# Softmax denominators in a fused attention and feed-forward kernel: one-hot matmuls replaced by row sums of exponentials taken on ScalarE

## What is computed

```python
def _L0_xattn_ref(q, k, v, wq, wk, wv, wo_w, wo_b):     # 16 heads of 32, window 128
    ...
    scores = jnp.einsum('bhnqd,bhnkd->bhnqk', qb, kband) * math.sqrt(dk)
    ...
    scores = jnp.where(valid[None, None], scores, neg)
    attn = jax.nn.softmax(scores, axis=-1)
    out = jnp.einsum('bhnqk,bhnkd->bhnqd', attn, vband)
    out = out.reshape(b, h, s, dk).transpose(0, 2, 1, 3).reshape(b, s, d)
    return jnp.einsum('bsd,ed->bse', out, wo_w) + wo_b
...
x = x + _L0_xattn_ref(_layernorm(x, axis=-1), ctx_1024, ctx_1024, ...)
x = x + _L0_ffn_ref(_layernorm(x, axis=-1), ...)         # 512 -> 2048 -> 512, quantised operands
```

## Time and profile before

| | |
|---|---|
| median of 3 runs | 1255.44 us (1254.12 to 1260.5) |
| the profiled execution | 1255.64 us |
| its span, first to last instruction | 1253.9 us |
| busy: PE, DVE, ACT, POOL | 1158.9, 985.8, 639.6, 367.9 us |
| granted TensorE clock, mean | 0.979 of full speed |

### The profile page before, as it was taken

How to read it: one execution, slowest core, us unless ns; L and a number is a source line. 1 busy time by engine, 2 the same in 40 slices (tenths; PEclk the granted TensorE clock), 3 DMA queues, 4 the chain that set the end, 5 groups by cost and what they waited for, 6 DMA issues and landing times.

```text
span 1253.9 us, 23541 instructions
## 1 busy us (share of the span) xinstructions
PE 1158.9 (92%) x7904; PEld 785.0 (63%) x7904; DVE 985.8 (79%) x2527; ACT 639.6 (51%) x1000; POOL 367.9 (29%) x540
## 2 busy tenths in 40 slices
PE   5789999999999999999999875999999979999997
PEld 5667877877887787787787653444444434444443
DVE  6779888889888888888988665666666678888885
ACT  5254355345335434533533443555556457777774
POOL 1136346345444624534554330000000030112320
PEclk9899999999999999999999887999999989999999
DMA  8463473465356347445534631455554400567662
GB/s 275 112 153 76 135 185 95 117 173 126 103 152 157 97 127 190 106 110 165 132 97 118 166 103 43 157 199 205 211 193 143 150 1 31 188 222 246 221 208 92
DMA packets 91592, 181.23 MB, mean 145 GB/s; under 512 B 12896, under 2 KB 22368, under 8 KB 91488
## 3 DMA queue, kind: packets, MB, share of 16 engines
q1 hardware_dynamic: 91488, 179.92, 48.1%
HBM read 81.30 MB, written 41.94 MB: 98 GB/s over the span
## 4 chain that ended last, share of the span: by engine, by line
DVE 36%; PE 35%; issue 25%; ACT 2%; DMA 1%; SPq 1%; POOL 0%; DVEq 0%; ACTq 0%; POOLq 0%
PE bank L787 17%; DVE bank L1059 7%; DVE roped L1085 3%; PE bank L505 3%; PE bank L506 3%; PE bank L507 3%; DVE bn L1020 3%; DVE rt L1082 3%; DVE rt L1083 3%; PE bank L594 2%; DVE row_max L1059 2%; DVE neg_max L1101 2%; PE bank L578 2%; DVE x_res L1052 1%; PE bank L517 1%
## 5 line engine op out<-in xcount | busy, mean ns | idle before, releaser
L1059 DVE CUSTOM_DVE_ANT_0 bank<-bank,mask 128x256 f32<-128x256 f32 x512 | 201.5, 454 | 63.7 <-PE bank L594 56.2
L787 PE MATMUL bank<-wout_int,g_hi 128*128 128x512 bf16 x512 | 195.7, 382 | 9.2 <-DVE g_lo L1332 9.2
L756 PE MATMUL bank<-qT_hi,win_int 128*128 128x512 bf16 x512 | 194.1, 379 | 1.6 <-DVE qT_lo L1250 1.4
L787 PE MATMUL bank<-wout_int,g_lo 128*128 128x512 bf16 x512 | 195.6, 382 | 0.0
L756 PE MATMUL bank<-qT_lo,win_int 128*128 128x512 bf16 x512 | 194.0, 379 | 0.0
L859 ACT ACTIVATE probs<-bank 128x512 f32<-128x512 f32 x256 | 142.5, 603 | 48.6 <-PE bank L621 44.2
L1377 POOL TENSOR_SCALAR_AFFINE_SELECT probs<-probs 128x256 f32<-128x256 f32 x256 | 109.6, 432 | 101.9 <-ACT probs L859 98.9
L1332 DVE TENSOR_TENSOR g_lo<-h_int,g_hi 128x512 f16<-128x512 f32 x128 | 103.7, 810 | 36.3 <-ACT g_hi L987 35.1
L594 PE MATMUL bank<-k_st,q_st 96*128 96x256 f32 x512 | 103.7, 309 | 19.7 <-DVE row_max L1059 11.6
L960 ACT ACTIVATE h_ring<-bank,b_in,g_scale 128x512 f32<-128x512 f32 x96 | 73.4, 779 | 75.7 <-PE bank L756 57.0
L1274 DVE TENSOR_REDUCE hmax<-h_ring 128x512 f32 (+1 forms) x96 | 63.2, 681 | 61.2 <-ACT h_ring L960 59.2
(11 more groups left out here) (148 smaller groups left out, 2783.3 us busy)
## 6 DMA issues: line engine op xcount, KB each, us to landing
hidden_scratch<-h_ring SPq DMA_DIRECT2D x96, 256.0 KB, 2.0
h_ring<-hidden_scratch SPq DMA_DIRECT2D x96, 256.0 KB, 2.9
k_st<-k_hi SPq DMA_DIRECT2D x128, 128.0 KB, 2.4
q_st<-q_hi SPq DMA_DIRECT2D x128, 128.0 KB, 2.4
xq<-x_scratch SPq DMA_DIRECT2D x16, 1024.0 KB, 6.0
x_ln<-in_x SPq DMA_DIRECT2D x16, 512.0 KB, 4.6
ctx_raw<-in_ctxT SPq DMA_DIRECT2D x16, 512.0 KB, 5.4
k_st<-k_lo SPq DMA_DIRECT2D x64, 128.0 KB, 2.5
```

Source lines behind the costliest of these rows:

```text
L756: mm = pe.matmul(bank[f % 4][:], win_int[:, c, f * P:(f + 1) * P], part[:, par, c], start=c == 0 and part is qT_hi, stop=c == KC - 1 and p ...
L787: mm = pe.matmul(bank[4 * par + u][:], part[:, f % 4, u * P:(u + 1) * P], wout_int[:, f], start=f == 0 and part is g_hi, stop=f == FC - 1 ...
L1059: dve.tensor_tensor_reduce(sc, sc, mask[:, (1 - qb) * P:(1 - qb) * P + S], 1.0, NEG, ALU.add, ALU.max, row_max[:, qb, n:n + 1]).then_inc(m ...
```

## The change

Three things are done. **The sums:** after the row maximum ACT takes the exponential of the first scores in place, one call for each half of the queries, with a running sum over the row into `den` (`sum_exp`, 32 calls a step); the first scores use four banks in place of two, and `denominators` and `hot` go. **The shares:** the 32 sums per row are inverted at once, `widen` copies each inverse 32 times (128x1024, into `roped`), and eight matmuls with the identity turn them (`shares`), now in the same step between `clump(1)` and the last four heads; ACT copies the shares instead of the output, and DVE multiplies straight from the output's bank at the end of the step. **The norm of x:** its chain (12 operations instead of 10, with the last one dropped into the norm) and the norm itself move to POOL, its moments to DVE's first part, after pair 4. The mask's constant, the sign of the maxima and the tables loaded follow.

```diff
+        first = [bank[i] for i in (0, 1, 6, 7)]
+        den_wide = roped[:].rearrange("p c s -> p (c s)").rearrange("p (q h r) -> p q h r", q=2, h=H)
# PE
             def x_transposes(j, s):
...
-                    wait(pe, den_done, j - 1)
+                    wait(pe, share_out, 2 * (j - 1))
...
-            def shares(j):
+            def shares(j, has_proj):
+                pe.wait_ge(den_done, j + 1)
+                if not has_proj:
+                    pe.wait_ge(wt_done, j)
                 for half in range(2):
-                    if half == 0:
-                        pe.wait_ge(den_done, j + 1)
-                    pe.wait_ge(oT_out, 2 * j + half + 1)
                     for a in range(2):
-                        mm = pe.matmul(pv_bank[half][:, a * S:(a + 1) * S], pick[:, 2 * half + a], den_r, start=True, stop=True)
+                        i = 2 * half + a
+                        for qb in range(2):
+                            mm = pe.matmul(q_bank[half][:, a * S + qb * P:a * S + (qb + 1) * P],
+                                           den_wide[:, qb, KC * i:KC * (i + 1)].rearrange("p h r -> p (h r)"), ident[:],
+                                           start=True, stop=True)
                     mm.then_inc(share_mm, 1)
...
             def scores(b, n):
...
+                elif n < 4:
+                    wait(pe, onorm, 2 * b)
                 else:
-                    pe.wait_ge(max_done, 2 * (H * b + n - 1))
+                    pe.wait_ge(sum_done, H * b + n - 3)
...
-            def denominators(b, i, kb, has_proj):
...
-                if has_o:
-                    tiles[2] += [lambda: shares(b - 1)]
-                    tiles[3] += [lambda: qk_tile(b + 1, "q", 0)]
...
+                    tiles[2] += [lambda: qk_tile(b + 1, "q", 0)]
+                    tiles[3] += [lambda: qk_tile(b + 1, "q", 1)]
+                    tiles[4] += [lambda: v_tile(b + 1, 0)]
+                    tiles[5] += [lambda: v_tile(b + 1, 1, range(2))]
+                    tiles[6] += [lambda: v_tile(b + 1, 1, range(2, KC))]
...
-                some(4)
-                max_transposes(b)
-                some(4)
-                for n, count in enumerate((1, 2, 2, 3, 1, 1, 1, 0, 1, 1, 1, 0, 1, 1, 0, 0)):
+                some(6)
+                max_transposes(b, has_proj)
+                some(6)
+                for n, count in enumerate((2, 2, 2, 2, 1, 1, 1, 1, 0, 0, 0, 0, 0, 0, 0, 0)):
                     scores_t(b, n, has_o)
                     some(count)
                     if n in (7, 11, 15):
-                        clump(b, par, n // KC - 1, has_proj)
+                        clump(b, par, n // KC - 1)
+                    if n == 11:
+                        shares(b, has_proj)
# ACT
+            def sum_exp(b, n):
+                act.wait_ge(max_done, 2 * (H * b + n + 1))
+                if n == 0:
+                    wait(act, den_chain, b)
+                for qb in range(2):
+                    sc = first[n % 4][:, qb * S:(qb + 1) * S]
+                    ins = act.activation(sc, sc, ACT.Exp, bias=row_low[:, qb, n:n + 1], scale=-1.0,
+                                         accum_out=den[:, qb, n:n + 1])
+                ins.then_inc(sum_done, 1)
...
             def step(b, par, has_c, has_o, has_proj, has_xt):
-                if has_proj:
-                    norm1(b + 1)
+                sums(0)
                 if has_proj:
                     xt_lead(b + 1, 0)
                     xt_lead(b + 1, 1)
+                sums(1)
+                sums(2)
+                sums(3)
                 if has_proj:
                     split_hi("k", b + 1)
+                sums(4)
                 if has_o:
                     ot_lead(b - 1, 0, has_proj)
                     ot_lead(b - 1, 1, has_proj)
+                sums(5)
                 if has_proj:
                     v_copy(b + 1, 1 - par, 0)
+                sums(6)
+                if has_proj:
                     v_copy(b + 1, 1 - par, 1)
+                sum_exp(b, 14)
                 max_copy(b, 0, slice(0, 2))
                 max_copy(b, 0, slice(2, KC))
+                sum_exp(b, 15)
                 for n in range(H):
                     softmax_exp(b, n)
...
-                    if n == 12:
-                        oT_copy(b, 0)
+                    if n == 13:
+                        share_copy(b, 0)
+                    if n == 14:
+                        share_copy(b, 1)
# DVE
             def invert(b):
-                dve.wait_ge(den_mm, NC4 * (b + 1))
+                dve.wait_ge(sum_done, H * (b + 1))
                 wait(dve, share_mm, 2 * b)
-                dve.reciprocal(den_r, den_bank[:, 0:S]).then_inc(den_done, 1)
+                dve.reciprocal(den_r[:], den[:]).then_inc(den_chain, 1)
+
+            def widen(b, has_proj):
+                dve.wait_ge(den_chain, b + 1)
+                if has_proj:
+                    dve.wait_ge(lo_done["q"], KC * (b + 2))
+                dve.tensor_copy(den_wide, den_r[:].rearrange("p q (h o) -> p q h o", o=1).to_broadcast([P, 2, H, DK])).then_inc(den_done, 1)
...
             def step(b, par, has_c, has_o, has_proj, has_xt):
...
-                if has_o:
-                    between[0] += [lambda: invert(b - 1)]
-                    between[5] += [lambda: normalise(b - 1, 0), lambda: normalise(b - 1, 1)]
...
+                if has_xt:
+                    between[4] += [lambda: ln1_moments(b + 2)]
...
+                invert(b)
...
                 quantise_win(b)
-                if has_xt:
-                    ln1(b + 2)
+                widen(b, has_proj)
                 if has_o:
                     residual(b - 1, 1)
                     ln2_moments(b - 1, 1)
+                normalise(b, 0)
+                if has_o:
                     largest(b - 1, 0)
                     largest(b - 1, 1)
+                normalise(b, 1)
# POOL
+            def norm1(j):
+                pool.wait_ge(ln1_chain, LN_SC * (j + 1))
+                for s in range(2):
+                    pool.tensor_scalar(x_ln[:, s], x_ln[:, s], mv[:, 0, s, 0:1], rstd[:, s:s + 1], ALU.subtract, ALU.mult).then_inc(ln1_norm, 1)
...
             def step(b, par, has_c, has_o, has_proj, has_xt):
+                if has_proj:
+                    norm1(b + 1)
                 if has_o:
                     bias_x(b - 1)
...
                     ot_rest(b - 1, 0)
                     ot_rest(b - 1, 1)
+                if has_xt:
+                    for _ in ln1_scale(b + 2):
+                        pass
                 for n in range(H):
                     band(b, n)
```

More of the change, by code:

```diff
@@ L73, in constants @@
     q, k = np.arange(S)[:, None], np.arange(S)[None, :]
-    mask = folded(folded(np.where(np.abs(q - k) <= WINDOW, 0.0, NEG).astype(np.float32), 0), 1)
+    mask = folded(folded(np.where(np.abs(q - k) <= WINDOW, 0.0, FAR).astype(np.float32), 0), 1)
     assert not mask[:P, :P].any() and not mask[P:, P:].any()
     mask = np.concatenate([mask[P:], mask[:P, P:]], 1)
-    hot = np.tile((np.arange(HOT) % NC4 == NC4 - 1).astype(np.float32), (P, 1))
-    row, col = np.arange(P)[:, None], np.arange(P)[None, :]
-    pick = np.stack([row == DK * (col // DK) + i for i in range(NC4)], 1).astype(np.float32)
     sel = np.zeros((P, H), np.float32)
@@ L810, in ctx_hi @@
                 act.copy(cT_hi[:], ctx_raw[:]).then_inc(c_hi, 1)
-            def norm1(j):
-                act.wait_ge(ln1_chain, LN1_OPS * (j + 1))
-                for s in range(2):
-                    act.activation(x_ln[:, s], x_ln[:, s], ACT.Identity, bias=nmr[:, s:s + 1],
-                                   scale=rstd[:, s:s + 1]).then_inc(ln1_norm, 1)
             def lead(src, s, done):
@@ L1022, in moments, with ln1_moments @@
                 link(dve.bn_aggr(mv[:, which, s], bn[:, which, s]))
-            def ln1(j):
+            def ln1_moments(j):
                 dve.wait_ge(xln_in, 16 * (j + 1))
-                link = chain(dve, ln1_chain, LN1_OPS * j)
+                wait(dve, ln1_chain, LN_SC * j)
+                link = chain(dve, ln1_moment, LN_ST * j)
                 moments(link, x_ln, 0, 0)
@@ L1120, in quantise_win @@
                 assert link.count[0] == WQ_OPS
-            ln1(0)
+            ln1_moments(0)
+            link = chain(dve, ln1_chain, 0)
+            for _ in rsqrt(dve, link, veps[:], rstd[:], nt_t[:]):
+                pass
+            assert link.count[0] == LN_SC
+            for s in range(2):
+                dve.tensor_scalar(x_ln[:, s], x_ln[:, s], mv[:, 0, s, 0:1], rstd[:, s:s + 1], ALU.subtract, ALU.mult).then_inc(ln1_norm, 1)
             dve.memset(neg_max[:], 0.0).then_inc(const_done, 1)
@@ L1370, in bias_x, with ln1_scale @@
                     pool.tensor_tensor(x_res[:, s], x_res[:, s], wo_b[:], ALU.add).then_inc(xres_b, 1)
+            def ln1_scale(j):
+                pool.wait_ge(ln1_moment, LN_ST * (j + 1))
+                link = chain(pool, ln1_chain, LN_SC * j, separate=True)
```

(12 more changed lines are left out.)

140 lines of the change are left out of this document (63 added, 77 removed).

## The result

| | before | after |
|---|---|---|
| median of the runs (us) | 1257.97 (4 runs, 1254.12 to 1261.39) | 1304.26 (4 runs, 1303.36 to 1310.23) |
| ratio to before, 95% interval | 1 | 1.0379 [1.0356, 1.0402] |
| profiled execution, its span (us) | 1255.64, 1253.9 | 1304.61, 1302.9 |
| first and last split of the maxima (us) | 66.7, 730.5 | 74.7, 776.7 |

The change is slower by 3.8%. The forecast was 1260 us with a range up to 1294: the measured time lies outside it. The profiled execution is 49.0 us longer than that of the kernel before. Each step has one split of the maxima, and the first and the last of them cut these 49.0 us in three: 8.0 ahead of the first, 38.2 between them (15 intervals), 2.8 behind the last.

A forecast was written before the change was run, and what follows sets the result against it. A loop of waits through PE, DVE, ACT and POOL bounds the kernel: a step of 24.0 + 12 x 0.48 + 15.8 = 45.6 us against 44.43, +16 over 14 steps, ends -12, from 1255.6: 1260 us, range 1234 to 1294.

The forecast's parts named there:

- moments between heads 9 and 10: Moments of the next x on DVE in the first part: 3.6 us, possibly 2.7 with uncontended small operations.
- one half of a sum: One `sum_exp` call on ACT: taken as 0.48 us, between 0.40 and 0.68; 12 halves for heads 10 to 15.
- first exponential: Start of ACT's exponentials, counted from the step's first scores: 24.0 + 12s = 29.8 us, against 27.7 before.
- tail: Second part, from the first exponential to the next step's first scores: 15.8 us, against 16.73 before.
- The ends: Step 14, step 15 and the stretch behind the last clump, with an unchanged prologue: together -12 us.
- The prologue exchanges equals.: The stretch ahead of the loop: claimed that what comes and what goes are equal, so no time was added.
- the chain of 12: The norm's small operations on POOL before the first band: 5.4 us at 0.45 each, under 7.8 us of cover.
- The norm on POOL: Between POOL's last bands and the transposes of x: at most 2.9 us, hidden under 6.4 us of cover.
- The busiest engine: Rival: the step shrinks by the 3.9 us that PE sheds, 1190 us with the ends; chance 0.13.
- The cheap variant: Rival: the loop holds, but moments take 2.7 and `widen` 0.7, 1.4 us a step less, 1240 us; chance 0.15.
- The dear sums: Rival: dearer sum halves between head 10's maximum and first exponential; 0.60 gives 1280 us, 0.68 gives 1293; chance 0.22.
- POOL's chain: Rival: POOL's 12 two-column operations take 1 us each, the bands start 4 us late, 1316 us; chance 0.05.

The follow-up runs named there:

- v_wait: The kernel after with one wait more: GpSimd holds the low parts of the outputs back until VectorE's moments are done; ratio to before 1.0123.
- k_end: The kernel after with GpSimd's low parts of the outputs put ahead of the bias in the last step alone; ratio to before 1.0302, 1300.1 us.
- w_all: The kernel after with both the wait of v_wait and the last step's order of k_end; ratio to before 1.0062.
- a_norm: The kernel after with the layer norm taken back from GpSimd: moments and chain on VectorE ahead of `widen`, norm on ScalarE; ratio to before 1.0307.
- h_home2: As a_norm, but with the moments behind `widen` and the second residual on VectorE; ratio to before 0.9924.
- d_one: The kernel before with one-hot products in the first clump only, the other heads' denominators left out; ratio to before 1.0057.
- l_hot: a_norm with ten matmuls of 128x512 more a step, which nobody reads, ahead of the shares; ratio to before 1.0174.
- r_warm2: The kernel after with twelve repeated V-tile matmuls of 128x512 more a step, ahead of TensorE's wait for scores 14; ratio to before 1.0386.

## Why the prediction was wrong

By its own steps, in us from the first scores of the step at 286.31 (the column of `v_wait` has means, and the moments of one step):

| step of the sum | predicted | after | v_wait |
|---|---|---|---|
| DVE starts head 4 | 8.4 | 8.18 | |
| end of heads 4 to 9 and the rotations | 17.5 | 17.29 | |
| moments between heads 9 and 10 | 3.6 | **5.23** | 3.05 |
| one half of a sum | 0.48 | 0.45 | |
| first exponential | 29.8 | 31.2 (mean 31.32) | 29.09 |
| POOL's fourth low part behind it | 7.8 | 8.37 | |
| `widen` | 1.2 | 0.83 | |
| shares | 1.7 | 1.81 | |
| tail | 15.8 | 16.33 (mean 16.25) | 16.22 |
| step | 45.6 | 47.54 | 45.3 |

The chain was right, and ACT behind head 10 was the link. **The failed step** is the sentence "Now stand the moments of the next x, with seed: 343.53 to 347.14, 3.6 us; uncontended small operations could make it 2.7." The duration came from another place in the step, with other work beside it: GpSimd operations of 0.4 and 0.7 us, beside which the three small operations took 0.41, 0.32 and 0.66 us instead of 0.17. Contention was taken in one direction only, as something that could go away, and what GpSimd does at 17.5 was not read. It is the low parts of the outputs, two operations of 1.27 us whose input ScalarE gives free at head 9. The term is 1.6 us larger than taken. `v_wait` removes the contention (3.05 us) and lands at a step of 45.3 against 45.6. Because the moments stand ahead of all the remaining maxima, no slack absorbed it: in 14 steps some 23 us. An earlier start of 0.2 and the cheaper sums, 12 x 0.03 = 0.4, give a little back; 0.4 ahead of the first exponential and 0.5 in the tail, where POOL's fourth low part alone comes 0.6 late, are left over.

**The ends** were taken as -12 us and came out as some +11 (8.0 and 2.8; the -12 also held 1.8 for step 14, which lies between the splits). Two statements failed. "now ACT needs 2.1 + 15 x 0.96 + 3.1 = 19.6" is the time to the first exponential in step 15: the kernel after took 27.5, since the price of ACT was worked out and GpSimd's queue was not, where a load that landed only at 779.16 stood ahead of the low parts. The kernel before had the same load ahead of them, at 727.14, and 24.4 us. With the order exchanged it is 19.8 in `k_end` and 19.3 in `w_all`. And "The prologue exchanges equals." was not worked out at all. GpSimd's chain for the second part starts with an operation on two columns that takes 2.20 us beside a VectorE subtraction of 2.29, where the eleven others take some 0.2: the same collision the other way round. Its two norms end 51.0 us into the run, and the transposes of x start at 51.07, where the kernel before had them at 45.95; TensorE is idle ahead of them and at half clock behind (rows of the kernel after):

```profile
40.09 2.29 DVE L1153 TENSOR_TENSOR wo_lo<-probs,wo_hi 128x2048 fp32r<-128x2048 f32 x1
40.24 2.20 POOL L283 TENSOR_TENSOR nt_t<-rstd 128x2 f32<-128x2 f32 x1 [0.41 <-DVE rstd L278]
46.84 4.17 POOL L1407 TENSOR_SCALAR x_ln<-x_ln,mv,rstd 128x512 f32<-128x512 f32 x2 [0.22 <-POOL rstd L289]
51.07 1.97 PE L518 MATMUL bank<-ident,x_ln 128*128 128x128 f32 x8 [3.55 <-POOL x_ln L1407]
```

`a_norm` and `h_home2`, which have the norm back, reach the first split at 67.9 and 66.9, against 74.7 here. No run changed the prologue alone, so how its 8.0 us divide stays open.

**What held.** The half of a sum, the chain of 12 (4.4 us, under its cover), the load of x, the shares, and `widen` waiting for the fourth low part (3.02 us before it starts). The norm on POOL, bounded by 1.46 a pass, takes 2.08 us; the cover held it in the loop. Of the signs, ACT worked without a pause and PE waited, as said; the first exponential, at 31.2, just missed its 29 to 31. Where the two terms are put right, the forecast's ratio of 1.0035 stands beside `w_all`'s 1.0062. Some of that nearness is luck: the prologue's 8 us were not in the sum, and the step of the kernel before was taken as 44.43 from one step, where the mean of its steps 1 to 14 is 44.64, so that `w_all`'s step (45.32) is 0.7 us longer and not 1.1.

**The rivals.** The busiest engine didn't decide (`d_one` sheds 2.9 us a step of it and gains nothing). The cheap variant had `widen` right (0.78 us against its 0.7) and the moments the wrong way. The dear sums had the right sign and the wrong term: the slower side was the place that they named, ACT behind head 10's maximum, only that what came late there was the maximum itself. POOL's chain did not run into the bands: it ends at 313.16, and the first band starts at 318.28. A GpSimd operation that holds up VectorE was no rival, and the range lacked it.

## What to carry to other kernels

When an operation is moved, its duration does not move with it: read in the new place what the other engines do at that moment, above all GpSimd beside VectorE's small operations on SBUF, and price both the alone and the blocked length. A queue's order in the first and last step deserves its own look, since a load that is covered in the loop is not covered there. A stretch at half clock is a reason to look, not a cause: fill the wait ahead of it with work that nobody reads, and see whether the time follows.

## What was unexpected of the hardware

- A `tensor_scalar` on 128x2 took 0.17 us with GpSimd idle and 1.31 beside GpSimd subtractions of 128x512 (1.27 each). The other way round, a GpSimd operation on 128x2 took 2.20 us instead of 0.2 beside a VectorE subtraction of 128x2048 (2.29).
- GpSimd's norm of 128x512, one tensor and two values per row, took 2.08 us, its subtraction with two tensors 1.27.
- Reading ScalarE's running sum shows as an instruction of 218 ns, but it starts 0.36 us after its exponential and the next exponential 0.09 after it (0.45 us a half). How short a half would be without the reading, no run shows.
- The granted clock went to half behind waits of TensorE of 2.05 us (after), 2.64 us (a_norm) and 1.31 us (d_one), for 3.4 us, and came back while it worked. Adding 160 matmuls made one kernel 1.3% faster (`l_hot`); adding 180 took nothing off and put nothing clear on another (`r_warm2`).
